# Turning the normalised input by DMA, with v's lo halves behind the second masks and a closing of its own

## The reference

```python
h = jnp.maximum(_layernorm(x, axis=-1), 0.0)          # x: (32, 256, 384)
q = _heads(h @ Wq + bq); k = _heads(h @ Wk + bk); v = _heads(h @ Wv + bv)
scores = jnp.einsum('bhqd,bhkd->bhqk', q, k) / np.sqrt(64)
probs = jax.nn.softmax(scores + jnp.where(adj, 0.0, -9e15)[:, None], axis=-1)
ctx = jnp.einsum('bhqk,bhkd->bhqd', probs, v)
out = x + ctx_joined @ Wf + bf
```

## Time and profile before

| | |
|---|---|
| median of three runs | 616.84 us (616.78 to 617.56) |
| profiled execution, its own time | 617.89 us |
| its span, first to last instruction | 616.0 us |
| mean granted TensorE clock | 0.989 of 2.4 GHz |
| busy: PE, ACT, POOL, DVE | 97%, 84%, 81%, 74% |
| one steady cycle | 17.93 us |

### The profile page before, as it was taken

The page is one execution under the profiler, slowest core; times in us unless marked ns, Lnnn a source line. Parts: engine busy times, 40 slices in busy tenths (PEclk is TensorE's granted clock), DMA queues, the critical chain, the costliest instruction groups (busy, mean ns, idle before and its releaser), DMA issues.

```text
span 616.0 us, 18008 instructions
## 1 busy us (share of the span) xinstructions
PE 596.3 (97%) x6806; PEld 451.9 (73%) x6806; DVE 456.9 (74%) x1479; ACT 516.5 (84%) x1166; POOL 496.1 (81%) x529
## 2 busy tenths in 40 slices
PE   7998999999999999999999999999999999999975
PEld 7666777777777777777777777777777777777753
DVE  5878777878777777877777787777778777776762
ACT  2688888889888889988888898888889888888980
POOL 2789888888888888888888888888888888888750
PEclk9998999999999999999999999999999999999997
DMA  8056766867766786666578767666886666765573
GB/s 264 6 100 117 133 124 128 157 128 146 139 139 122 129 159 127 145 131 150 118 129 159 130 141 134 142 123 129 159 136 136 140 141 121 126 133 112 100 136 80
DMA packets 232280, 81.14 MB, mean 132 GB/s; under 512 B 214273, under 2 KB 232194, under 8 KB 232194
## 3 DMA queue, kind: packets, MB, share of 16 engines
q1 hardware_dynamic: 230992, 79.99, 66.1%
q10 hardware_dynamic: 1202, 0.01, 0.1%
HBM read 17.05 MB, written 12.58 MB: 48 GB/s over the span
## 4 chain that ended last, share of the span: by engine, by line
PE 87%; ACT 6%; DVE 2%; DMA 2%; issue 1%; POOL 1%; ACTq 0%; DVEq 0%; POOLq 0%
PE ring L858 19%; PE ring L860 19%; PE ring L859 19%; PE scores L922 11%; PE ctx L939 5%; PE ring L951 4%; PE ctx L940 3%; PE ctx L941 3%; PE ring L874 3%; ACT probs L479 2%; DMA bf_row<-in_L_gnn_bf_dram 1%; ACT qk L496 1%; ACT p_rows L484 1%; DMA p_cols<-p_rows 1%; PE ring L981 1%
## 5 line engine op out<-in xcount | busy, mean ns | idle before, releaser
L379 POOL TENSOR_TENSOR p_rows<-probs,p_rows 128x512 f16<-128x512 f32 x192 | 222.4, 1158 | 58.5 <-ACT p_rows L484 57.3
L632 DVE CUSTOM_DVE_ANT_0 logits<-scores,mask,logit_unscale 128x256 f32<-128x256 f32 x384 | 169.1, 477 | 39.0 <-PE scores L922 37.1
L479 ACT ACTIVATE probs<-logits,raised 128x256 f32<-128x256 f32 x384 | 174.3, 500 | 6.2
L858 PE MATMUL ring<-h_hi,w_hi 128*128 128x256 f16 x576 | 157.7, 274 | 0.6 <-DVE h_lo L640 0.6
L860 PE MATMUL ring<-h_hi,w_lo 128*128 128x256 f16 x576 | 157.5, 273 | 0.0
L859 PE MATMUL ring<-h_lo,w_hi 128*128 128x256 f16 x576 | 157.4, 273 | 0.0
L365 POOL TENSOR_TENSOR split<-qk,split 128x512 f16<-128x512 f32 x96 | 111.0, 1157 | 25.2 <-DVE split L648 25.2
L484 ACT ACTIVATE p_rows<-probs 128x512 f16<-128x512 f32 x192 | 121.0, 630 | 6.1
L496 ACT ACTIVATE qk<-ring,qk_bias_s,qkv_ratio 128x256 f32<-128x256 f32 x192 | 96.3, 551 | 3.9 <-PE ring L860 3.9
L939 PE MATMUL ctx<-v_hi,p_cols 128*128 128x65 f16 x768 | 90.7, 196 | 7.4 <-DMA p_cols<-p_rows 4.4
L939 PEld LDWEIGHTS ctx<-v_hi,p_cols 128*128 128x128 f16 x768 | 70.2, 97 | 33.4 <-issue 23.6
(11 more groups left out here) (89 smaller groups left out, 1222.2 us busy)
## 6 DMA issues: line engine op xcount, KB each, us to landing
x_in<-in_x_dram SPq DMA_DIRECT2D x32, 384.0 KB, 3.9
out_dram<-result SPq DMA_DIRECT2D x64, 192.0 KB, 2.2
p_cols<-p_rows SPq DMA_TRANSPOSE x192, 3.1
adj_in<-in_adj_dram SPq DMA_DIRECT2D x32, 64.0 KB, 2.6
w_raw<-in_L_gnn_Wq_dram SPq DMA_DIRECT2D x1, 576.0 KB, 5.8
w_raw<-in_L_gnn_Wv_dram SPq DMA_DIRECT2D x1, 576.0 KB, 7.9
w_raw<-in_L_gnn_Wf_dram SPq DMA_DIRECT2D x1, 576.0 KB, 9.1
w_raw<-in_L_gnn_Wk_dram SPq DMA_DIRECT2D x1, 384.0 KB, 6.8
```

What stands on the lines that cost most here:

```text
L379: pool.tensor_tensor(p_rows[u][:, 1], probs[u % 3][:], p_rows[u][:, 0], ALU.subtract).then_inc(p_lo_ready, 1)
L479: act.activation(probs[u % 3][:, a], logits[u % 3][:, a], ACT.Exp, bias=raised[u % 3][:, a:a + 1], scale=-1.0).then_inc(probs_ready, 1)
L632: dve.tensor_tensor_reduce(out=logits[u % 3][:, a], in0=score_bank[a][:, u % 2 * S:(u % 2 + 1) * S], in1=mask[b.parity][:, t], scale=logit ...
L858: pe.matmul(out_ap, a_hi, m_hi, start=first, stop=False)
```

## The change

1. Batches 2 to 31 are no longer turned on TensorE. ScalarE makes the high half straight from `normed` into a row tile `h_rows` (`h_hi_rows`, two activations of 128 x 384), VectorE the low half (`h_lo_rows`, two instructions of 128 x 384), and SP turns both by one DMA transpose of 128 x 1536 fp16, twelve blocks, into `h_cols` (`transpose_h` of SP). Batches 0 and 1 are turned as before (`BY_PE = 2`). The work for batch b+2 is done in `cycle(b)`.
2. `v_lo_part(b, 0)` leaves the end of cycle b-1 on VectorE and stands behind `mask_and_max(b, 1)` in cycle b.
3. The raise of the extremum in the cycle is left on ScalarE. In the closing it is on GpSimd.
4. The generic cycle runs for b = 1 to 30. What follows is written out for each engine. The last two units of batch 31 are turned on TensorE (`turn_probs`, four fp32 transposes each) with `turned_hi` on ScalarE and `turned_lo` on VectorE instead of by DMA, and the last half of the output is made in two parts.

The core of the diff, in the order SP, ScalarE, VectorE, TensorE:

```diff
+            def transpose_h(b):
+
+                wait(sp, h_lo_ready, b.count(2, 2))
+                sp.dma_start_transpose(h_cols[b.parity][:].rearrange("p w c (t k) -> p (w c t) k", k=P),
+                                       h_rows[:].rearrange("p w c t n -> p (w c t n)")).then_inc(h_placed, 16)
...
                 if here:
                     transpose_probs(b, 1)
+                if (b + 2).exists():
+                    transpose_h(b + 2)
                 if here:
                     transpose_probs(b, 2)
...
+            def h_hi_rows(b):
+                wait(act, h_placed, (b.k - BY_PE) * 16)
+                for t in range(QT):
+                    wait(act, norm_ready, b.count(2, t + 1))
+                    act.activation(h_rows[:, 0, :, t], normed[:, t].rearrange("p (c n) -> p c n", n=P),
+                                   ACT.Relu).then_inc(h_hi_ready, 1)
...
-                if front:
-                    h_hi_part(b + 1)
...
                 if front:
                     qk_full(b + 1, 0)
+                if (b + 2).exists():
+                    h_hi_rows(b + 2)
...
+            def h_lo_rows(b):
+                for t in range(QT):
+                    wait(dve, h_hi_ready, b.count(2, t + 1))
+                    dve.scalar_tensor_tensor(
+                        out=h_rows[:, 1, :, t], in0=normed[:, t].rearrange("p (c n) -> p c n", n=P),
+                        scalar=0.0, in1=h_rows[:, 0, :, t], op0=ALU.max, op1=ALU.subtract).then_inc(h_lo_ready, 1)
...
                 if before:
                     divide(b + -1, 0)
-                if front:
-                    h_lo_part(b + 1)
 
                 if here:
                     mask_and_max(b, 1)
                 if here:
+                    v_lo_part(b, 0)
                     v_lo_part(b, 1)
...
                     context_lo(b + -1, 0)
+                if (b + 2).exists():
+                    h_lo_rows(b + 2)
...
-                if front:
-                    v_lo_part(b + 1, 0)
...
                 attend(0)
-                if front:
-                    transpose_h(b + 1)
                 if (b + -2).exists():
                     project_out(b + -2, 1)
...
+            scores(LAST, 0)
+            apply_probs(PREV, 2)
+            project_out(PREV + -1, 1)
+            apply_probs(PREV, 3)
+            scores(LAST, 1)
...
+            turn_probs(4)
+            apply_probs(LAST, 1)
+            turn_probs(5)
+            apply_probs(LAST, 2)
+            project_out(PREV, 1)
...
+            apply_probs(LAST, 5)
+            project_out(LAST, 0)
+            project_out_last(UP_TO, 2)
+            transpose_context_last(FROM, 3)
+            project_out_last(FROM, 3)
```

More of the change, by code:

```diff
@@ L239, in wait, with ctx_of @@
                 eng.wait_ge(s, value)
+        LAST, PREV = Batch(B - 1), Batch(B - 2)
+        last_pt = {4: ring[2], 5: score_bank[0]}
+        UP_TO, FROM = slice(0, 2), slice(2, 3)
+        def ctx_of(b, t):
+            bank = peak_bank if b.k == B - 1 and t == 0 else ctx_bank
+            return bank[:, 0:HEADS * V1].rearrange("p (h d) -> p h d", h=HEADS)
         def pair(j):
@@ L336, in _, with store_last @@
             transpose_probs(Batch(0), 3)
+            transpose_h(Batch(2))
             cycles(cycle)
+            def store_last(t):
+                sp.wait_ge(result_ready, LAST.count(2, t + 1))
+                sp.dma_start(out_v[LAST.k, t], normed[:, t]).then_inc(out_stored[t], 16)
+            transpose_probs(PREV, 4)
+            store(PREV + -1, 0)
+            transpose_probs(PREV, 5)
+            transpose_probs(LAST, 0)
+            store(PREV + -1, 1)
+            for u in (1, 2, 3):
+                transpose_probs(LAST, u)
+            store(PREV, 0)
+            store(PREV, 1)
+            store_last(0)
+            store_last(1)
             for t in range(QT):
@@ L466, in _, with raise_last @@
             cycles(cycle)
+            def raise_last(u):
+                pool.wait_ge(logits_ready, LAST.count(2 * UNITS, 2 * u + 2))
+                pool.tensor_scalar(raised[u % 3][:], least[u % 3][:], P_RAISE, None, ALU.add).then_inc(raised_ready, 1)
+            probs_lo(PREV, 5)
+            raise_last(0)
+            raise_last(1)
+            probs_lo(LAST, 0)
+            raise_last(2)
+            probs_lo(LAST, 1)
+            raise_last(3)
+            probs_lo(LAST, 2)
+            raise_last(4)
+            probs_lo(LAST, 3)
+            raise_last(5)
         @block.scalar
@@ L558, in _ @@
             qk_full(Batch(1), 2)
+            h_hi_rows(Batch(2))
             exps(Batch(0), 4)
@@ L609, in _, with exps_last, turned_hi, context_hi_last @@
             cycles(cycle)
+            def exps_last(u):
+                act.wait_ge(raised_ready, LAST.count(UNITS, u + 1))
+                act.wait_ge(p_lo_ready, LAST.count(UNITS, u - 2))
+                for a in range(2):
+                    act.activation(probs[u % 3][:, a], logits[u % 3][:, a], ACT.Exp,
+                                   bias=raised[u % 3][:, a:a + 1], scale=-1.0).then_inc(probs_ready, 1)
+            def turned_hi(u, nth):
+                act.wait_ge(pt_ready, nth)
+                act.activation(p_cols[u][:, 0].rearrange("p a s q -> p (a s q)"), last_pt[u][:],
+                               ACT.Copy).then_inc(pt_hi_ready, 1)
+            def context_hi_last(chunks, nth):
+                act.wait_ge(ct_ready, LAST.count(2, nth))
+                act.activation(ct_hi[1][:, chunks].rearrange("p c q -> p (c q)"),
+                               R_CT[1][:, chunks.start * P:chunks.stop * P], ACT.Copy).then_inc(ct_hi_ready, 1)
+            exps_last(0)
+            probs_hi(LAST, 0)
+            v_hi_part(LAST, 1)
+            exps_last(1)
+            probs_hi(LAST, 1)
+            exps_last(2)
+            probs_hi(LAST, 2)
+            context_hi(PREV, 0)
+            exps_last(3)
+            probs_hi(LAST, 3)
+            exps_last(4)
+            exps_last(5)
+            turned_hi(4, 1)
+            context_hi(PREV, 1)
+            turned_hi(5, 2)
+            context_hi(LAST, 0)
+            context_hi_last(UP_TO, 2)
+            context_hi_last(FROM, 3)
         @block.vector
@@ new lines, in context_lo_last, with finish_last @@
+            def context_lo_last(chunks, nth):
+                dve.wait_ge(ct_hi_ready, LAST.count(2, nth))
+                dve.tensor_tensor(ct_lo[1][:, chunks].rearrange("p c q -> p (c q)"),
+                                  R_CT[1][:, chunks.start * P:chunks.stop * P],
+                                  ct_hi[1][:, chunks].rearrange("p c q -> p (c q)"),
+                                  ALU.subtract).then_inc(ct_lo_ready, 1)
+            def finish_last(t):
+                dve.wait_ge(out_ready, LAST.count(2, t + 1))
+                dve.wait_ge(residual_ready, LAST.count(2, t + 1))
+                dve.scalar_tensor_tensor(out=normed[:, t], in0=R_OUT[t][:, 0:H], scalar=out_unscale[:, 0:1],
+                                         in1=residual[LAST.slot][:, t], op0=ALU.mult,
+                                         op1=ALU.add).then_inc(result_ready, 1)
@@ new lines, in _ @@
+            mask_and_max(LAST, 0)
+            mask_and_max(LAST, 1)
+            divide(PREV, 0)
+            v_lo_part(LAST, 0)
+            v_lo_part(LAST, 1)
+            mask_and_max(LAST, 2)
+            mask_and_max(LAST, 3)
+            finish(PREV + -1, 1)
+            context_lo(PREV, 0)
+            mask_and_max(LAST, 4)
+            mask_and_max(LAST, 5)
+            divide(PREV, 1)
+            finish(PREV, 0)
+            turned_lo(4, 1)
+            context_lo(PREV, 1)
+            divide(LAST, 0)
@@ L854, in _ @@
+            turned_lo(5, 2)
+            finish(PREV, 1)
+            divide_last(UP_TO, 5, 2)
+            context_lo(LAST, 0)
+            context_lo_last(UP_TO, 2)
+            divide_last(FROM, 6, 3)
+            context_lo_last(FROM, 3)
+            finish_last(0)
+            finish_last(1)
         @block.tensor
@@ L877, in project_qk @@
             def project_qk(b, j, parts=(0, 1)):
-                if j == 0:
+                if j == 0 and b.k < BY_PE:
                     wait(pe, h_lo_ready, b.count(2, 2))
+                elif j == 0:
+                    wait(pe, h_placed, (b.k - BY_PE + 1) * 16)
+                if j == 0 and (b + -3).exists():
+                    wait(pe, ct_lo_ready, (b + -3).count(2, 2))
                 if j == 1 and (b + -3).exists():
@@ L928, in apply_probs @@
                 t, j = u // C, u % C
-                wait(pe, p_placed[u], b.count(16, 16))
+                ctx_ps = ctx_of(b, t)
+                if b.k == B - 1 and u >= 4:
+                    pe.wait_ge(pt_lo_ready, u - 3)
+                else:
+                    wait(pe, p_placed[u], b.count(16, 16))
                 if u == 0:
                     wait(pe, v_lo_ready, b.count(2, 2))
-                if j == 0:
+                if b.k == B - 1 and u == C:
```

(39 more changed lines are left out.)

50 lines of the change are left out of this document (34 added, 16 removed).

## The result

The changed kernel takes 695.0 us (median of 4 runs, 693.57 to 696.32) against 616.97 us before: a ratio of 1.126, 95% interval 1.124 to 1.129. That is slower by 78 us. The forecast was 687 us, from 671 to 700. The profiled execution took 696.32 us with a span of 694.5 us and a mean granted clock of 0.958.

What follows compares the result with a forecast made beforehand. The prediction took TensorE, busy 97% of the span, as the bound. Span 616.0 + 60.6 (wait) + 14 (clock) - 1 (opening) - 3.4 (closing) = 686.2 us, so 687 us expected, range 671 to 700.

Steps and rivals of the forecast that it cites:

- The wait: Head of each generic cycle: project_out on TensorE waits 2.78 us for v_lo; cycle 20.02 us, 60.6 us more in all.
- The clock: After the stalls in the cycles: one in three followed by low clock, 10 x 1.4 = 14 us more.
- the rival in which the clock never falls: Steady cycles: the stall comes as forecast but the clock stays up, 673 us; chance 0.15.
- The rival in which it falls at nearly every stall: Steady cycles: low clock after nearly all 29 stalls, 43 us instead of 14, 716 us; chance 0.08.
- What replaces the transposes: Steady cycle: new ScalarE and VectorE pieces and SP's twelve-block DMA transpose cost 0 on the path, at most 0.5 a cycle.
- Opening and closing: First cycle and end of the kernel: -1 us (bounds -3 and +2) and 3.4 us less (bounds 0 and 7).
- The rival of a hidden wait: Head of each cycle: v_lo's wait is hidden and TensorE gains its transposes, 590 us; chance 0.05.
- The rival of a late DMA in each cycle: Each cycle: apply_probs or project_qk waits for DMA, adding perhaps 1 us a cycle, 715 us; chance 0.03.
- 20.7 us of transposes: TensorE, batches 2 to 31: removing the fp32 transposes gives at most 30 x 0.69 = 20.7 us, taken alone.

Runs made afterwards that it cites:

- e1: The changed kernel with v's first lo half put back at the end of the cycle on VectorE, ahead of the first masks: 614.8 us, ratio 0.998.
- e2: The kernel before with one edit alone, v's first lo half moved behind the second masks on VectorE: 768.5 us, ratio 1.246.
- e6: The changed kernel with v's first lo half directly behind the first masks, ahead of divide, in the cycle: 631.4 us, ratio 1.025.
- e8: The changed kernel with 11 unused matmuls of zeros on TensorE ahead of the waiting project_out in the generic cycle: 675.0 us, ratio 1.096.
- e10: e7 with the closing of before: generic cycle to 33, last two units turned by DMA: 597.5 us, ratio 0.971.
- e9: The changed kernel with the closing of before: generic cycle to 33, last two units turned by DMA: 696.2 us, ratio 1.130.
- e7: The changed kernel with v_lo directly behind divide on VectorE, and q and k first, then project_out, then apply_probs on TensorE: 596.5 us, ratio 0.968.

## Why the prediction was right, point by point

**The wait.** Right in place, releaser and size. Forecast: TensorE waits 2.78 us for v_lo and a cycle takes 20.02 us. Measured: 2.66 us of idle time, which is 316.17 - 313.35 = 2.8 us from the time at which it was free, and 20.06 us. Each link of the chain (0.04, 0.81, 0.70, 0.81, 0.62, 0.1) is in the timeline after within 0.05. e1 shows that undoing the edit removes the loss, e2 that the edit alone makes one, e6 that its size goes with VectorE's list ahead of v_lo. The term was 60.6 us and measured 29 x (20.06 - 17.93) = 61.8.

**The clock.** The mechanism was right, and the term was mis-sized: 10 stretches of 1.4 us, 14 us, against 13 longer cycles and 21.1 us. That is 7.1 of the 8.3 us by which the span came out above the forecast. The pattern was mostly one in three, as chosen, and since no row gave one in three, that is luck in part. Eight of the longer cycles cost 1.3 us more than a plain one, but three cost 1.65 and two 2.9 us. In the longest shown, the clock was low for (1 - 0.85) x 22.96 / 0.5 = 6.9 us, twice the length that I took from the earlier trace rows. e8, which fills the wait, has the clock up and all cycles at 20.06 us; by it the term is 19 us, and its 675.0 us are close to the 673 of the rival in which the clock never falls. The rival in which it falls at nearly every stall was near as well: in e2 the wait was only 0.3 us longer, and 27 of the 29 profiled cycles had low clock. The Trainium skill (TensorE: Matmul & The Clock Gate, Why this matters for your kernels) warns that idle gaps between matmul bursts lower the clock in mid-kernel. This trace agrees in that, with a mean clock of 0.85 in such a cycle, but the gaps of 2.66 us are shorter than those that the page warns of.

The prediction counted three idle times in the trace of before and two falls. There is a fourth, of 2.00 us, and the clock is at 0.50 soon after it. From the timeline of TensorE and a window of the kernel before:

```profile
11.56 0.65 PE L973 MATMUL peaks<-ident,peak 128*128 128x128 f32 x4 [2.00 <-DVE peak L744]
```

```profile
12.67:16.08 3.41, 3.41 (x18) 3.41 (x18) 3.20 (x12) 2.01 (x4) 1.89 (x7) 0.50 0.72 241
```

So an idle time of 2.00 us went with a fall and one of 1.87 us did not (the window of it in the earlier trace rows ends only 0.25 us behind it, but the clock stays at 1.00 from there to 603.00), and the length of the idle time alone does not tell: of 29 waits of 2.66 us, 13 cycles had low clock and 16 had none.

**What replaces the transposes.** Right that it costs nothing in the steady cycle. ScalarE's pair took 0.93 us (1.0 taken), the DMA transpose of twelve blocks landed after 4.3 us by the median (4.7 taken, 3.7 to 5.5), from these rows of the kernel after, the groups by form and the DMA issues:

```profile
L757 DVE SCALAR_TENSOR_TENSOR h_rows<-normed,h_rows 128x384 f16<-128x384 f32 x60 | 43.2, 759 | 0.0
L557 ACT ACTIVATE h_rows<-normed 128x384 f16<-128x384 f32 x60 | 27.9, 518 | 0.0
...
h_cols<-h_rows SPq DMA_TRANSPOSE x30, 4.3
```

The only wait of TensorE for the new transpose is the 0.71 us in the first cycle. VectorE's pieces were dearer than taken, 759 ns each against 0.55 us, hidden like the rest. It goes with what GpSimd does at the same time. The pair on VectorE and GpSimd's `split` beside it, first in the changed kernel, then in e1:

```profile
302.83 1.40 DVE L757 SCALAR_TENSOR_TENSOR h_rows<-normed,h_rows 128x384 f16<-128x384 f32 x2
302.19 1.16 POOL L408 TENSOR_TENSOR split<-qk,split 128x512 f16<-128x512 f32 x1 [2.77 <-DVE split L764]
```

```profile
310.50 1.03 DVE L757 SCALAR_TENSOR_TENSOR h_rows<-normed,h_rows 128x384 f16<-128x384 f32 x2
309.49 1.16 POOL L408 TENSOR_TENSOR split<-qk,split 128x512 f16<-128x512 f32 x1 [0.36 <-DVE split L764]
```

`split` covers 302.83 to 303.35 of the slow pair, 0.52 us, and 0.15 us of the fast one: the more of the pair it covers, the longer the pair takes. No run was made to vary this alone.

**Opening and closing.** Forecast -1 and -3.4 us. Measured, from the chains of the profiles: -0.4 (batch 2's scores at 64.81 against 65.23) and -3.3 (26.9 us from the last batch's scores; the windows above give 3.2). That the closing came out so near is luck in part: the new order gives 2.0 to 2.5 us of it in e10 and e9, and the lower clock of before in that stretch goes with the rest. One cycle of the kernel before was 0.7 us longer than the others, which is saved too. The sum closes: 616.0 + 61.8 + 21.1 - 0.4 - 3.3 - 0.7 = 694.5 us.

**The other side.** The rival of a hidden wait gave 590 us for v_lo early enough. e1 shows a gap in that rival: with v_lo ahead of the first masks TensorE still waits 0.60 us, and the masks wait for v_hi, 614.8 us. Its time is neared only with both orders changed, 596.5. The prediction had said of v_hi only that it is ready in time, and did not ask whom v_lo holds up when it waits for v_hi. The rival of a late DMA in each cycle is refuted: such a wait stands in the first cycle alone (0.71 us, and 4.30 us in e7) and in none after it, not even at 17.3 us.

## What to carry to other kernels

Before an instruction is moved down its engine's list, look for the instruction that waits for it on another engine, and add up all that now stands ahead of it from the event that starts that list; here five durations from one timeline gave the wait to 0.1 us. When work is taken off the bounding engine, ask which loop of hand-overs is next before counting the gain: 20.7 us of transposes gave almost nothing (614.8 us in e1) until both v_lo's place and TensorE's order had been changed. If an engine must wait, give it independent work to issue first, as e7 does with q and k.

## What the runs showed of the hardware

Matmuls of zeros into a spare bank kept the clock at 1.00 in the cycles through a wait of 2.7 us and so made the kernel about 19 us faster than the same kernel without them (675.0 against 695.0; 19 by the ratios). Eight turned blocks of 128 x 128 landed 3.2 us after issue and twelve after 4.3 by the medians of the changed kernel; in e7, where the DMA share went up to 0.88, it was 3.2 and 4.8. The two h_rows pieces of VectorE took 1.40 us together where GpSimd's `split` covered 0.52 us of them and 1.03 where it covered 0.15. In the profile of e2, with waits of 2.95 us, 27 of 29 cycles had low clock, and with 2.7 us 13 of 29; about 60 us of loss beside 21. Why that step is so large, these runs do not settle.
